# One weight load, x by partition, tiles normed half a block later, a low half one slot later

## The reference

```python
# x: (2048, 512), adj: (2048, 2048), weight: (512, 512)
xq = act_quant(layernorm(x)); wq = weight_quant((weight - mean) / std)
support_q = act_quant(relu(xq @ wq * scales))
x = x + (adj / s) @ (support_q / d) * s * d

xn = layernorm(x)
probs = softmax(xn @ Wr + br);  topk_w, topk_idx = top_k(probs, 2)
h = gelu(layernorm_e(xn @ W1[e] + b1[e]))     # e: 16 experts, 512 -> 512
y = h @ W2[e] + b2[e]                         # 512 -> 512
x = x + sum of the two chosen y, weighted
```

## Time and profile before

| | us |
|---|---|
| three runs, median (lowest to highest) | 530.51 (530.3 to 532.35) |
| the profiled execution | 533.4 |
| its span, first to last instruction | 531.6 |
| TensorE busy | 480.7 (90%) |
| VectorE busy | 352.1 (66%) |
| ScalarE busy | 289.3 (54%) |
| GpSimd busy | 218.9 (41%) |

### The profile page before, as it was taken

The page is one execution under the profiler, slowest core; times in us unless marked ns, Lnnn a source line. Parts: engine busy times, 40 slices in busy tenths (PEclk is TensorE's granted clock), DMA queues, the critical chain, the costliest instruction groups (busy, mean ns, idle before and its releaser), DMA issues. The chain is left out here.

```text
span 531.6 us, 10328 instructions
## 1 busy us (share of the span) xinstructions
PE 480.7 (90%) x2328; PEld 392.9 (74%) x2329; DVE 352.1 (66%) x732; ACT 289.3 (54%) x484; POOL 218.9 (41%) x269
## 2 busy tenths in 40 slices
PE   0699999899999996678999999999999999999981
PEld 0488888788878775657788788888777888778851
DVE  5798856556567568848665786676878766776420
ACT  1666543443342342516667667668768766666540
POOL 3364411411351726234445444444345444344432
PEclk9999999999999999559999999999999999999997
DMA  8721222765787441155766776766887896644433
GB/s 262 267 80 48 82 89 81 237 208 172 244 284 253 150 171 50 35 159 203 237 161 151 186 212 154 218 166 148 239 282 198 252 270 170 136 84 81 80 60 41
DMA packets 33177, 87.75 MB, mean 165 GB/s; under 512 B 6048, under 2 KB 6192, under 8 KB 33152
## 3 DMA queue, kind: packets, MB, share of 16 engines
q1 hardware_dynamic: 19056, 56.53, 33.0%
q0 software_dynamic: 9488, 22.55, 21.1%
q10 hardware_dynamic: 4608, 8.39, 4.2%
HBM read 68.05 MB, written 19.40 MB: 164 GB/s over the span
## 5 line engine op out<-in xcount | busy, mean ns | idle before, releaser
L864 ACT ACTIVATE g_sb<-ps,be_sb,g_sb 128x128 f32<-128x128 f32 x160 | 60.2, 458 | 64.0 <-PE ps L1488 64.0
L624 POOL DMA_INDIRECT xg<-xn_rows,tok_i x41 | 44.2, 1079 | 114.4 <-ACT gate L843 94.8
L1227 DVE TENSOR_TENSOR w_lo<-w_raw,w_hi x58 | 67.8, 1221 | 16.5 <-issue 16.5
L966 DVE SCALAR_TENSOR_TENSOR adj_lo<-adj_raw,small,adj_hi 128x1024 fp32r<-128x1024 f32 x32 | 40.8, 1273 | 39.8 <-ACT adj_hi L704 39.6
L649 POOL DMA_INDIRECT out<-y_sb,scat_i x37 | 58.7, 1586 | 19.1 <-issue 11.0
L836 ACT ACTIVATE w_hi<-w_raw x29 | 54.8, 1914 | 0.7
L1234 DVE TENSOR_SCALAR h_hat<-ps,h_mv,h_rs 128x512 f32<-128x512 f32 x40 | 32.3, 807 | 29.7 <-issue 15.3
L1332 PE MATMUL ps<-sup,adj_hi 128*128 128x512 f32 x192 | 49.7, 401 | 2.2 <-ACT adj_hi L704 2.2
L580 POOL TENSOR_SCALAR rstd<-mv 128x1 f32<-128x1 f32 x15 | 13.7, 912 | 92.4 <-DVE mv L1012 92.4
L1332 PE MATMUL ps<-sup,adj_lo 128*128 128x512 f32 x192 | 49.7, 401 | 0.0
L1216 DVE BATCH_NORM_STATS2 h_stats<-ps 128x6 f32<-128x512 f32 x40 | 27.8, 696 | 28.1 <-PE ps L1472 28.0
(11 more groups left out here) (181 smaller groups left out, 951.3 us busy)
## 6 DMA issues: line engine op xcount, KB each, us to landing
w_raw<-in_w SPq DMA_DIRECT2D x64, 512.0 KB
adj_raw<-in_adj_steps SPq DMA_DIRECT2D x32, 512.0 KB, 3.5
out<-x_sb ACTq DMA_DIRECT2D x16, 256.0 KB, 3.0
xn_rows<-xn ACTq DMA_DIRECT2D x16, 256.0 KB, 2.9
x_sb<-in_x SPq DMA_DIRECT2D x3, 1024.0 KB, 13.3
gw_raw<-in_gnn_w SPq DMA_DIRECT2D x2, 512.0 KB, 5.9
x_sb<-in_x SPq DMA_DIRECT2D x2, 512.0 KB, 8.5
xg<-xn_rows,tok_i POOLq DMA_INDIRECT x41, 5.9
```

The source lines that it names most:

```text
L624: return pool.indirect_dma_start(to[:, s % 2, :], None, xn_rows, bass.IndirectOffsetOnAxis(ap=tok_i[:, s:s + 1], axis=0)).then_inc(landed[ ...
L864: ins = act.activation(g_sb[:, par, c * P:(c + 1) * P], ht_ps(par)[:, c * P:(c + 1) * P], ACT.Gelu, scale=g1_sb[:, bass.ds(e_s * C + c, 1) ...
L966: dve.scalar_tensor_tensor(adj_lo[:, par, :], adj_raw[:, par, :], small[:, 0:1], adj_hi[:, par, :].bitcast(F32), ALU.mult, ALU.subtract).t ...
L1227: ins = dve.tensor_tensor(w_lo[:, n, at], w_raw[:, n, :, :].rearrange("p a n -> p (a n)")[:, at], w_hi[:, n, at].bitcast(F32), ALU.subtract)
```

## The change

- The graph weight comes in one load with one semaphore; the wait for it stands ahead of the four statistics.
- x is laid out on the host so that each partition's share of a load is one run in memory; the five loads stay.
- Tiles from 5 on are normed and copied one window later and transposed and routed one half-step later; the routers of tiles 0 to 3 come one half-step later. Tile 14 is normed, transposed and routed, and tile 13's bias added, behind the windows.
- In the expert slots VectorE makes the low half of the layer-two weight one slot later, between g_lo and x_lo, and reads the plan word before the current one too.

```diff
 def transposed_after(t):
-    return (2, 3, 5, 6, 9)[t] if t < 5 else 4 * (t - TQ) + (7 if t < T - 2 else 6)
+    return (2, 3, 5, 6, 9)[t] if t < 5 else 4 * (t - TQ) + 8
 def routed_after(t):
-    return transposed_after(t) + 1
+    return transposed_after(t) + (2 if t < 4 else 1)
 def normed_in(t):
-    return t + 1 if t < 5 else 2 * (t - TQ) + 3
+    return t + 1 if t < 5 else 2 * (t - TQ) + 4
 def copied_in(t):
-    return (2, 3, 4, 4, 6)[t] if t < 5 else 2 * (t - TQ) + 4
+    return (2, 3, 4, 4, 6)[t] if t < 5 else 2 * (t - TQ) + 5
@@ SyncE
-            for i in range(2):
-                at = slice(i * 2 * D, (i + 1) * 2 * D)
-                sp.dma_start(gw_raw[:, at], gnn_w[:, at]).then_inc(gw_in[i], 16)
+            sp.dma_start(gw_raw[:, :], gnn_w).then_inc(gw_in, 16)
-                sp.dma_start(x_sb[:, t0:t0 + n, :],
-                             x[t0 * P:(t0 + n) * P, :].rearrange("(t p) d -> p t d", p=P)).then_inc(x_in[i], 16)
+                sp.dma_start(x_sb[:, t0:t0 + n, :].rearrange("p t d -> p (t d)"),
+                             x[:, t0 * D:(t0 + n) * D]).then_inc(x_in[i], 16)
@@ ScalarE, behind the windows
+            norm_xn(T - 2)
+            store_xn(T - 2)
+            gate_exp(3)
             finish_t(T - 2)
-            gate_exp(3)
@@ VectorE
+            dve.wait_ge(gw_in, 16)
             for c in range(C):
-                if c % 2 == 0:
-                    dve.wait_ge(gw_in[c // 2], 16)
                 ins = dve.bn_stats(stats[:, c, :], gw_raw[:, c * D:(c + 1) * D])
...
+            add_br(T - 3)
             pick(3)
...
-            def slot(s, par, word):
+            def slot(s, par, word, earlier):
                 slot_h_hat(s + 1, 1 - par)
                 slot_g_lo(s, par)
+                if earlier is not None:
+                    split_next(1, expert_in(earlier, 1 - par), starts_in(earlier, 1 - par))
                 slot_x_lo(s + 3, 1 - par)
                 slot_stats(s + 2, par)
                 split_next(0, expert_in(word, par + 2), starts_in(word, par + 2))
-                split_next(1, expert_in(word, par), starts_in(word, par))
...
-                    word = load_plan(dve, j)
+                    earlier, word = load_plan(dve, j - 1), load_plan(dve, j)
                     for par in range(2):
-                        slot(j * 2 + par, par, word)
+                        slot(j * 2 + par, par, word, word if par else earlier)
...
-            word = load_plan(dve, rest + 1)
+            earlier, word = load_plan(dve, rest), load_plan(dve, rest + 1)
             slot_h_hat(rest * 2 + 3, 1)
             slot_g_lo(rest * 2 + 2, 0)
+            split_next(1, expert_in(earlier, 1), starts_in(earlier, 1))
             split_next(1, expert_in(word, 0), starts_in(word, 0))
@@ TensorE, in and behind the windows
-                for t in range(T - 1):
+                for t in range(T - 2):
                     if routed_after(t) == hs:
                         router(t)
...
+            finish_t(T - 2)
             rank(3)
             finish_t(T - 1)
+            router(T - 2)
             router(T - 1)
@@ host
-        "x": np.asarray(x),
+        "x": np.ascontiguousarray(np.asarray(x).reshape(T, P, D).transpose(1, 0, 2).reshape(P, T * D)),
```

More of the change, by code:

```diff
@@ L302, in gnn_moe_program @@
         small_in = sem("small_in")
-        gw_in = [sem(f"gw_in{i}") for i in range(2)]
+        gw_in = sem("gw_in")
         x_in = [sem(f"x_in{i}") for i in range(len(X_LOADS))]
@@ L1261, in _ @@
             split_next(0, expert_in(word, 1), starts_in(word, 1))
-            slot(0, 0, word)
-            slot(1, 1, word)
+            slot(0, 0, word, None)
+            slot(1, 1, word, word)
             with dve.Fori(1, SLOTS // 2 - 1) as j:
```

## The result

| | kernel before | changed kernel |
|---|---|---|
| median of the runs, us | 530.46 (530.3 to 532.35, 4 runs) | 521.53 (520.81 to 522.36, 4 runs) |
| ratio, 95% interval | | 0.9832 (0.9807 to 0.9856) |
| profiled execution: time, span, us | 533.4, 531.6 | 522.36, 520.6 |

What follows compares the result with a forecast made beforehand. TensorE bounds the windows and expert slots, chains of short steps the rest. Terms 6.2 + 1.7 + 0.3 - 1.0 + 5.0 - 0.5 = 11.7 us give 521.7 from the profiled 533.4; against the median, less 0.7, 519.5; range 515.5 to 525.5.

Steps and rivals of the forecast that it cites:

- The clock's fall in the windows: Granted clock of 0.66 at 103 to 108 us, put down to two close copy waits; 1.7 us gained, bounds 0 and 1.7.
- (c): Rival at the start: larger runs bring weight and x earlier, 1.4 us gained instead of 0.5 lost; 517.6 us, chance 0.08.
- (b): Rival in the windows: ScalarE's queue only changes what it stands before, half of 7.9 us stays; 523.5 us, chance 0.11.
- (e): Rival: the moves cancel, windows give 3, experts 2, start and gap take 3; 528.5 us, chance 0.04.
- Start: Before the first product: VectorE's statistics wait for the whole weight, about 8.39 us; 0.5 us lost, bounds 0 and 1.0.
- Windows: Second product's windows: TensorE's waits for adj_hi, copied and normed tiles go, 6.2 us gained; tile 14's transposes move, 0.3.
- Gap: Behind the windows, VectorE waits for router 14: 1.0 us lost, bounds 0.5 and 1.5; clock shift 0, 1.5 either way.
- Slots: Expert slots: seven meetings of layer-one and layer-two low halves, with h_hat waits, go for 6.1 us; 0.9 is left.
- Loads: Expert weight loads leave some 2.5 us later, but ScalarE asks for them only two to three slots on.
- End: Behind the expert loop: one more plan word on VectorE's path to h_hat, 0.2 us lost, bounds 0 and 0.6.
- Rival (a): Expert slots: splitting a meeting does not help, six new meetings each cost 0.90 us; 524.0 us, chance 0.15.
- (d): Rival in the expert slots: VectorE stands for a late layer-two high half, 15 us lost; 534.5 us, chance 0.03.

Runs made afterwards that it cites:

- edit 1 alone: The kernel before with only the graph weight in one load and x laid out by partition: 529.43 us (ratio 0.9967).
- the other router order: The changed kernel with router 14 ahead of the transposes of tile 15 on TensorE (two calls swapped): 520.29 us (ratio 0.9804).
- Edit 3 alone: The kernel before with only layer two's low half one slot later on VectorE, in the expert slots: 528.11 us (ratio 0.9953).

## Why the prediction was right, point by point

The median came out at 521.53, 2.0 above the forecast of 519.5 and inside the range. The total is right partly because errors cancel: the start was 2.5 us better, the slots and their end 3.8 worse, the way from the gather to the first expert 1.3 better. Against the profiled execution it was 0.7 off (521.7 and 522.36). The other 1.3 comes from the change of yardstick: the profiled execution of before was 2.9 us above its median and that of the changed kernel 0.8, and the forecast had taken off only 0.7. The clock's fall in the windows (1.7) and the late start (0.8) would be 2.5 of the 2.9. Of the rivals (c) happened in its mechanism beside the forecast; (b) fell, since 0.7 of the 7.9 us of waits is left, and so did (e).

- **Start: wrong sign.** The step that failed is "with one load all four statistics start when the whole weight is there, about 8.39". That landing was of one execution, and of two loads. The one load's last byte is there before 6.3 us, earlier than the first half in the earlier trace rows, and x is there by 9. The profile's page gives 5.9 us from issue to landing for each half and 5.0 for the whole. The 393 GB/s of the earlier trace rows was no argument: it is the rate at 12 us, and the start hung on the time to 9 us, where the one load brought 292 to 303 GB/s (2 to 6 us) in place of 210 to 245. The Trainium skill, "Perfetto Trace Analysis", DMA Optimizations, has both the rule for larger transfers and the one for splitting; here the traces agree with the first.
- **Windows: right.** The waits and transposes were 6.2 + 0.3 us. Between two kernels whose clock stays up in this stretch, edit 1 alone and the changed one, it is 173.02 - 166.72 = 6.3. The wait left over is 0.7, not 0.4. The clock's 1.7 us was in the profiled execution; if it was not in the median one, it should have been taken off whole, not by 0.7. Its cause as I put it, the two copy waits close together, fell as a sufficient one: edit 1 alone had both and no fall. Three of the four traces with all six waits have the fall and none of the ten others, so what decides it stays open.
- **Gap: right.** 1.25 us longer for the 1.0 forecast (0.85 to 1.35 over the seven traces), and one swapped call brings it back to 18.98. The wait was 1.83, above the bound of 1.5: the clock had already fallen when router 14 started at 202.04, and its eight products, half of the 3.44 us, ended near 203.8. From the gather to the first expert it is 1.3 us less, inside the 1.5 either way; from 8 to 13 us behind the first gather the granted clock was 0.78 in the kernel before, and in the changed kernel it is 1.00 from 8 us on.
- **Slots: the mechanism right, one term mis-sized.** By the slot lengths the seven meetings cost 6.0 us; the sum had 6.1. All seven went. The failed step is the rest that was to be left, "I price the wait at 0.45 each, 0.9 together (bounds 0 and 1.8)": 3.1 us are left, in slots 21 to 24 and 27 to 28. The places were wrong too. The sum named the 20th and the 25th slot; the 20th takes 6.85 us, and 2.3 of the 3.1 us lie in slots 22 and 23, behind the halves of 373.25, 377.94 and 381.54, for which the sum says "No wait". I had counted VectorE's work and left out two tops of the loop that fall into this chain: VectorE's (2.60 us between the statistics' end and h_hat) and TensorE's (2.75 us after a late low half). With the first moved, slot 22 falls to 6.88; that TensorE's top makes slot 23 is read from the equal distances in nine traces, and no run moved it. "The second plan word and the added branch fall beside TensorE work in the loop" fails just there.
- **Loads: "ScalarE asks for them two to three slots on" fell.** ScalarE waits 5.1 us in all, one of the signs that the prediction named for being wrong. The order of the loads took the waits away and slots 22 to 24 stayed as long, so the waits were not what made them long.
- **End: size.** The second word costs 0.36 us (4.69 against 4.33), inside 0 to 0.6, but the longer wait was followed by a fall of the clock in the changed kernel's trace, 1.4 us more than in the trace with the other router order. Edit 3 alone had the longer wait (4.70) and no fall, and its end takes 15.81 us.
- **Rival (a)** fell for single meetings; **(d)** did not occur in the changed kernel, where VectorE stood once, 0.6 us, for a high half. The half behind the statistics shows a loss of another kind: there a late low half stops TensorE, and the time is the kernel before's.

## To carry to other kernels

Before one landing time or a fallen clock goes into a sum, ask whether it is in the median run too; two traces of the same stretch show it at once. When work moves on an engine inside a loop, add the loop's top to its chain, and on TensorE too wherever the last wait of the body is late. Work split off a busy point must be checked for the new time at which it is wanted, not only for the time that it frees.

## What the runs showed of the hardware that I had not expected

GpSimd's issue of a scatter takes longer in most cases when VectorE works on a low half. In the kernel before none of the 37 scatters runs beside a low half, and all take 1.57 to 1.66 us, and in the changed kernel up to 2.54, with the same median. Page groups of before and after:
```profile
L649 POOL DMA_INDIRECT out<-y_sb,scat_i x37 | 58.7, 1586 | 19.1 <-issue 11.0 <-DMA out<-y_sb,scat_i 8.1
```
```profile
L647 POOL DMA_INDIRECT out<-y_sb,scat_i x37 | 65.7, 1776 | 21.7 <-DMA out<-y_sb,scat_i 11.4 <-issue 10.3
```
The eleven scatters that overlap a low half take 2.20 us in the mean, seven of them 2.3 to 2.5; the others take 1.60, none over 1.78. Two of one trace, with VectorE's work beside the second:
```profile
353.28 1.58 POOL L647 DMA_INDIRECT out<-y_sb,scat_i  x1 [0.30 <-issue]
...
360.39 2.52 POOL L647 DMA_INDIRECT out<-y_sb,scat_i  x1 [0.31 <-issue]
...
359.11 2.35 DVE L1227 TENSOR_TENSOR w_lo<-w_raw,w_hi  x2
```
The low half reads two tensors in SBUF, and the scatter takes its row numbers, `scat_i`, from there. The Trainium skill, "SBUF — State Buffer", section "SBUF: two separate sides", says that such a VectorE operation and a GpSimd operation that reads SBUF exclude each other for a whole instruction; this trace agrees in kind, with up to 0.9 us more. No run here changes one of the two operations alone, so the cause is argued. The 7.0 us that the scatters grew by lie on GpSimd, which mostly had the time.
